# A three-stage decoder layer on one Trainium2 core: six cross-attention units in the last self-attention batch, the loop over key heads written out, and the maxima of heads 6 and 7 ahead of the rotations

## The chip, the cores and the metric

The kernel runs on one core of a Trainium2 chip. The metric is the device time of one execution in microseconds (us). The engines are PE (TensorE, the matrix engine), DVE (VectorE), ACT (ScalarE), POOL (GpSimd) and SP (SyncE, which here only issues transfers). Each runs its own list of instructions in order; they wait for each other at semaphores.

## The reference, cut to what matters

The input x is 8 sequences of 128 tokens by 512 features; ctx has the same shape.

```python
x = x + self_attention(layernorm(x))            # 32 query heads, 8 key heads of 16, causal, rotary positions
x = x + cross_attention(layernorm(x), ctx)      # keys and values from concat(ctx, latents): 256 keys
                                                # 32 query heads, 4 key heads of 128
x = x + ffn(layernorm(x))                       # up/ReLU^2/down, plus a latent path times the two best gates
```

In the cross-attention, `q = latents @ Wq`, `k, v = concat(ctx, latents) @ Wk, Wv`, a softmax over 256 keys, the sum over values, and `@ Wo`. Everything is float32. The kernel splits each operand into a high and a low part and makes three products (high by high, high by low, low by high).

## The kernel before, in words

**The split.** `split3` (lines 218 to 220) issues the three matmuls of one product. A result in a PSUM bank is turned into its two parts by ACT (`hi`, a copy, line 1033) and then DVE (`lo`, the difference, line 1280); weights that come from memory get their low part on POOL (`lo_part`, line 496). So a product that feeds another one passes PE, ACT, DVE, PE.

**Stage one, self-attention.** `batch(b, last)` on each engine runs eight batches. A batch goes over eight key heads j: `turn(j)` transposes the normalised probabilities Pa on PE (line 713), ACT and DVE split them into PTah and PTal, `values(j)` multiplies by the values on PE. Ahead of that, `scores(b, m)` makes the scores of two heads (mask by identity at line 681, then Kbdh by QTh, Kbdh by QTl, Kbdl by QTh at lines 685, 687, 690), DVE takes the maxima (`maxima`, line 1401), ACT the exponentials (`probs`, line 1088), DVE the reciprocals of the sums (`reciprocals_a`, line 1407), POOL multiplies (`normalise`, line 505). Inside batch b the queries and keys of batch b + 1 are made: `q_product`, `kv_product`, the rotary rotation on DVE (`rope_q`, lines 1339 to 1348, `rope_k_parts`, `rope_k_sum`, line 1358), `turn_qk`, and the block diagonal of the keys (Kbdh on POOL, line 490, Kbdl on DVE, line 1376). At the end of a batch the output product with SOh, the residual (line 1453), the second layer norm (xn2, line 1459) and `turn_latents` (line 650), whose result enters the tile XT.

**Units.** A "unit" is one 128 x 512 block of keys or values for the cross-attention: twelve matmuls on PE (`unit`), a copy (`unit_hi`) and a difference (`unit_lo`) into one of four slots of KVst, and a store to kv_scratch by SP (`store_unit`, two transfers). There are 32: units with part 0 need only the context, those with part 1 need latents, v of batch b only those of b, k those of four batches. The list UNITS gives their order and bank: five at the start, two in each batch (after head 0 and after the output product), and the eleven of `U_END` behind the last batch.

**Between the stages.** Behind batch 7 PE waits for the latents, runs the eleven units, then the first eight `queries` of cross-attention (WQh, WQl; split by `first_wq` on ACT and `first_wq_lo` on POOL), waits for the last unit's low part, and makes `scores_b(0, 0)` and `scores_b(0, 1)`.

**Stage two, cross-attention.** `group(g, last)` is run for four key heads g; g = 0 to 2 by a hardware loop (`Fori`) on each engine, g = 3 by a copy of its own. A group has 32 steps k: `scores_b(g, k + 2)`, the transposes of step k (line 925), from k = 8 on a piece of the output product of the batch before (`out_piece`), `queries` of the next pair of batches, `outputs(g, k - 1)`. ACT does in a step: PTh, `probs_b` (line 1170), `split_weights(k)` (WOh, at k = 0 twice, at k = 1 once), at odd k `queries` (Qh), `outputs` (Oh). DVE takes maxima (line 1513) and their negative (b_nb, line 1516).

**Stage three** is the feed-forward part, a loop over pairs of batches. The change does not touch it.

Of the kernel before, what the change touches and what calls it, by code (L numbers as in the profile page):

```python
# [34 lines left out]
NB = 8  # L35
# [25 lines left out]
def decoder_layer(nc, x, ctx, s_wq, s_wk, s_wv, s_wo, x_wq, x_wk, x_wv, x_wo, gate_w, up_w, down_w,  # L61
                  fc1_w, fc2_w, expert_w, gamma, beta, rope, out):
    with ExitStack() as stack:
# [239 lines left out]
        def targets(kind, i):  # L303
# [19 lines left out]
        U_END = [("v", b, None, 1, (0, 1, 7, 6)[b % 4]) for b in range(1, NB)] + [  # L323
            ("k", 1, g, 1, (0, 1, 7, 6)[g]) for g in range(XKV)]
        UNITS = U_START + U_BATCH + U_END
        NU = len(UNITS)
        U_B0, U_E0 = len(U_START), len(U_START) + len(U_BATCH)
# [14 lines left out]
        def _(sp):  # L342
# [37 lines left out]
            for n in range(U_E0 - 4):  # L380
                store_unit(n)
# [5 lines left out]
            for n in range(U_E0 - 4, U_E0):  # L387
                store_unit(n)
            sp.wait_ge(pe_pv, NB)
            sp.dma_start(gate_raw[:], gate_w.rearrange("(k p) n -> p k n", p=P)).then_inc(ld_gate, 16)  # L390
            for n in range(U_E0, U_E0 + 2):
                store_unit(n)
            stored(U_E0 + 2)
            for b in range(3):
                sp.dma_start(f32(KV[:, b, :]), kv_scratch[0, b]).then_inc(b_kv[b], 16)

            sp.wait_ge(pe_ht, NB)
# [13 lines left out]
            def group(g, last):  # L411
# [4 lines left out]
                for k in range(DUOS):  # L416
# [8 lines left out]
                    if k == 26 and not last:  # L425
                        first_loads(sp.snap(g + 1))
                    for done, gg, b in kv_loads:
                        if done == k + 1:

                            n = NB * gg + b if last else sp.snap(NB * gg + b)  # L430
                            sp.wait_ge(b_pe_pv, DUOS * g + done)
                            sp.dma_start(f32(KV[:, b % 3, :]), kv_scratch.rearrange("g b p n -> (g b) p n")[n]
                                         ).then_inc(b_kv[b % 3], 16)

            with sp.Fori(0, XKV - 1) as g:
                group(g, False)
            group(XKV - 1, True)
# [18 lines left out]
        def _(gp):  # L456
# [118 lines left out]
            with gp.Fori(0, XKV - 1) as g:  # L575
                group(g, False)
            group(XKV - 1, True)
# [18 lines left out]
        def _(pe):  # L596
# [73 lines left out]
            def scores(b, m):  # L670
# [6 lines left out]
                else:  # L677

                    pe.wait_ge(v_qkl, 2 * b + 2)
# [4 lines left out]
                for bk, rows in halves:  # L684
                    pe.matmul(bk[:], QTh[rows, m, :], Kbdh[rows, m, :], start=False, stop=False)  # L685
                for bk, rows in halves:
# [5 lines left out]
            def queries(g_count, head, pair, bk):  # L692
# [8 lines left out]
                op.then_inc(b_pe_q, 1)  # L701

            def batch(b, last):
# [31 lines left out]
                for j in range(SKV):  # L735
# [27 lines left out]
                    if j == 7 and not last:  # L763
                        turn_qk(b + 1)
                    if j >= 1:
                        values(j - 1)
                values(SKV - 1)
                if not last:

                    pe.wait_ge(a_exp, SKV * b + SKV)  # L770
                    scores(b + 1, 0)

# [8 lines left out]
                unit(U_B0 + 2 * b + 1)  # L781
# [3 lines left out]
                else:  # L785

# [917 lines left out]
```

## Time and profile before

| | us |
|---|---|
| median of 3 runs (lowest, highest) | 1091.8 (1091.32, 1091.91) |
| the profiled execution, its own time | 1089.78 |
| its span, first to last instruction | 1088.1 |

| engine | busy us | share of the span |
|---|---|---|
| PE (matmul) | 1038.0 | 95% |
| DVE | 639.1 | 59% |
| ACT | 546.5 | 50% |
| POOL | 387.0 | 36% |

In order of time: the start up to about 50 us, the eight self-attention batches to about 302, units and first queries to about 347, four cross-attention groups to about 948, the feed-forward part to the end. How to read a row of a timeline: start, duration, engine, line of the kernel, operation, output from input, shape, count; in brackets the idle time of the engine just before it and who ended it. Matmul ends are modelled: consecutive matmuls overlap in the rows, so the spacing of two starts is the time that one costs, and real waiting is a little more than the bracket says.

### The profile page before, as it was taken

Reading aid. Unit: us, or ns where it says so; the run is one execution under the profiler, and the core shown is the slowest. Engines: PE = TensorE matmul, PEld = TensorE weight load, DVE = VectorE, ACT = ScalarE, POOL = GpSimd, SP = SyncE. Lnnn points to the kernel's source line nnn. Section 1 sums busy time; section 2 is a strip of 40 time slices with the busy share of each in tenths; the row PEclk is TensorE's granted clock in tenths of the full one; section 3 lists DMA queues with packets and bytes.
Section 4 is the critical chain, followed back from the end, with each engine's and each line's share of the span. In section 5 each row is a group of like instructions: output and inputs, shape, how many; then the busy total and the mean of one; then the engine's idle time right before and its main releaser. Section 6 shows DMA issues by size and latency. Waiting matters only on the chain.

```text
span 1088.1 us, 19297 instructions
## 1 busy us (share of the span) xinstructions
PE 1038.0 (95%) x6808; PEld 920.3 (85%) x6808; DVE 639.1 (59%) x1369; ACT 546.5 (50%) x1657; POOL 387.0 (36%) x370
## 2 busy tenths in 40 slices
PE   5899999999899999998999998999999999999997
PEld 5667777776678999998999998999999999899996
DVE  5677787787524655555555554555546555655554
ACT  4566666656623645644545544546546446622221
POOL 2454444444331523423424414324316235611110
PEclk9999999999999999999999999999999999999999
DMA  9301111104164212121102302103112123200000
GB/s 329 93 25 40 39 39 40 32 13 113 39 201 129 59 31 77 50 78 51 49 30 59 107 24 59 37 30 107 59 40 59 35 73 97 78 21 19 19 20 20
DMA packets 70123, 68.64 MB, mean 63 GB/s; under 512 B 3984, under 2 KB 53904, under 8 KB 70032
## 3 DMA queue, kind: packets, MB, share of 16 engines
q1 hardware_dynamic: 70032, 67.43, 19.8%
q8 instruction: 56, 0.92, 0.4%
q14 instruction: 35, 0.29, 0.1%
HBM read 48.55 MB, written 18.87 MB: 62 GB/s over the span
## 4 chain that ended last, share of the span: by engine, by line
PE 83%; DVE 7%; ACT 5%; POOL 2%; issue 2%; DMA 1%; SPq 0%; POOLq 0%; DVEq 0%; ACTq 0%
PE bank L218 24%; PE bank L220 23%; PE bank L219 23%; PE bank L925 5%; PE bank L713 2%; PE bank L681 1%; ACT Pa L1088 1%; PE bank L685 1%; POOL Pa L505 1%; DVE PTal L1280 1%; ACT PTah L1033 1%; DVE b_nb L1516 1%; ACT Pb L1170 1%; DVE b_max L1513 1%; PE bank L690 1%
## 5 line engine op out<-in xcount | busy, mean ns | idle before, releaser
L543 POOL TENSOR_TENSOR Pb<-Pb,b_rec 128x512 f32<-128x512 f32 x128 | 133.3, 1042 | 406.0 <-DVE b_rec L1520 405.7
L218 PE MATMUL bank<-XTh,WQh 128*128 128x256 f32 x512 | 146.5, 286 | 3.8 <-DVE Ql L1280 3.8
L220 PE MATMUL bank<-XTh,WQl 128*128 128x256 f32 x512 | 145.9, 285 | 0.0
L219 PE MATMUL bank<-XTl,WQh 128*128 128x256 f32 x512 | 145.7, 285 | 0.0
L1170 ACT ACTIVATE Pb<-bank,b_nb 128x256 f32<-128x256 f32 x256 | 119.2, 471 | 30.1 <-DVE b_nb L1516 29.2
L1033 ACT ACTIVATE PTh<-bank 128x512 fp32r<-128x512 f32 x128 | 76.8, 600 | 104.8 <-PE bank L925 104.6
L1280 DVE TENSOR_TENSOR Ol<-bank,Oh 128x256 fp32r<-128x256 f32 x128 | 53.8, 420 | 117.7 <-ACT Oh L1033 117.6
L1088 ACT ACTIVATE Pa<-bank,a_nb 128x128 f32<-128x128 f32 x256 | 90.7, 372 | 51.8 <-DVE a_nb L1401 51.7
L505 POOL TENSOR_TENSOR Pa<-Pa,a_rec 128x512 f32<-128x512 f32 x64 | 70.5, 1101 | 114.5 <-DVE a_rec L1407 114.5
L218 PE MATMUL bank<-WOh,Oh 128*128 128x512 f32 x256 | 109.9, 429 | 1.0 <-DVE x_res L1530 1.0
L218 PEld LDWEIGHTS bank<-XTh,WQh 128*128 128x128 f32 x512 | 98.5, 192 | 9.5 <-DVE Ql L1280 4.8
L219 PEld LDWEIGHTS bank<-XTl,WQh 128*128 128x128 f32 x512 | 98.6, 193 | 4.6
L220 PE MATMUL bank<-WOh,Ol 128*128 128x512 f32 x256 | 101.0, 395 | 0.0
L219 PE MATMUL bank<-WOl,Oh 128*128 128x512 f32 x256 | 100.8, 394 | 0.0
L220 PEld LDWEIGHTS bank<-XTh,WQl 128*128 128x128 f32 x512 | 98.7, 193 | 0.0
L1033 ACT ACTIVATE Oh<-bank 128x256 fp32r<-128x256 f32 x128 | 49.2, 384 | 96.6 <-PE bank L220 90.5
L1280 DVE TENSOR_TENSOR Ql<-bank,Qh 128x512 fp32r<-128x512 f32 x64 | 44.3, 692 | 84.7 <-ACT Qh L1033 84.7
L1280 DVE TENSOR_TENSOR PTl<-bank,PTh 128x512 fp32r<-128x512 f32 x128 | 88.2, 689 | 9.9 <-ACT PTh L1033 1.1
L1513 DVE TENSOR_REDUCE b_max<-bank 128x2 f32<-128x512 f32 x128 | 87.2, 681 | 10.6 <-PE bank L220 10.6
L218 PE MATMUL bank<-KV,Qh 128*128 128x256 f32 x256 | 73.3, 286 | 7.1 <-issue 5.2
L925 PE MATMUL bank<-ident,Pb 128*128 128x128 f32 x512 | 76.9, 273 | 0.3 <-POOL Pb L543 0.3
L220 PE MATMUL bank<-KV,Ql 128*128 128x256 f32 x256 | 73.0, 285 | 0.0
(230 smaller groups left out, 2866.9 us busy)
## 6 DMA issues: line engine op xcount, KB each, us to landing
kv_scratch<-KVst SPq DMA_DIRECT2D x64, 256.0 KB, 3.0
KV<-kv_scratch SPq DMA_DIRECT2D x32, 512.0 KB, 3.3
raw<-in_L_xattn_Wo_dram SPq DMA_DIRECT2D x32, 256.0 KB, 3.6
raw<-in_L_xattn_Wq_dram SPq DMA_DIRECT2D x24, 256.0 KB, 4.0
cx<-in_ctx_dram SPq DMA_DIRECT2D x8, 256.0 KB, 8.6
raw_first<-in_L_xattn_Wq_dram SPq DMA_DIRECT2D x8, 256.0 KB, 4.5
raw<-in_L_ffn_up_w_dram SPq DMA_DIRECT2D x8, 256.0 KB, 4.1
raw<-in_L_ffn_down_w_dram SPq DMA_DIRECT2D x8, 256.0 KB, 2.7
```

The source lines that it names most:

```text
L218: pe.matmul(dst, lh, rh, start=start, stop=False)
L219: pe.matmul(dst, lh, rl, start=False, stop=False)
L220: return pe.matmul(dst, ll, rh, start=False, stop=stop)
L505: gp.tensor_tensor(pj, pj, a_rec[:, SG * j:SG * j + SG].unsqueeze(2).to_broadcast([P, SG, P]), ALU.mult).then_inc(g_norm, 1)
L543: gp.tensor_tensor(pk, pk, b_rec[:, k % 4, :].unsqueeze(2).to_broadcast([P, 2, KEYS]), ALU.mult).then_inc(b_g_norm, 1)
L713: op = pe.transpose(bank[5 + j % 2][:, c * P:(c + 1) * P], Pa[:, j % PS, c * P:(c + 1) * P], ident[:])
L925: op = pe.transpose(bank[3 + k % 2][:, c * KEYS + h * P:c * KEYS + (h + 1) * P], Pb[:, k % 4, h, c * P:(c + 1) * P], ident[:])
L1033: return act.activation(dst, src, ACT.Copy)
L1088: op = act.activation(Pa[:, j % PS, c * P:(c + 1) * P], bank[2 + j % 3][:, c * P:(c + 1) * P], ACT.Exp, bias=a_nb[:, h:h + 1], scale=1.0, ...
L1170: op = act.activation(Pb[:, k % 4, h, :], bank[k % 3][:, h * KEYS:(h + 1) * KEYS], ACT.Exp, bias=b_nb[:, k % 4, h:h + 1], scale=X_SCALE, a ...
L1280: return dve.tensor_tensor(dst, src, f32(hi_part), ALU.subtract)
L1513: dve.tensor_reduce(b_max[:, k % 4, :], bank[k % 3][:].rearrange("p (h k) -> p h k", h=2), AX.X, ALU.max).then_inc(b_v_mx, 1)
```

## The change: what it does, and the diff

1. `UNITS` is reordered. Of the eleven last units six (values of batches 1 to 6, part 1) now stand in batch 7, at heads 2, 4, 5, 6, 7 and after the last head (`LAST_STEPS`), in banks 0 and 1 by turns; five stay behind the batch. The stores, the loads of KV and the waits of SP follow the new order.
2. On PE the eight first queries are put between other work: heads 0 and 1 before the last `turn_latents`, 2 and 3 before the five last units, 4 and 5 before `scores_b(0, 0)`, 6 and 7 before `scores_b(0, 1)`. Waits are moved to where they are needed, on ACT and DVE likewise (the stores' end is waited for in `outputs(0, 0)`).
3. `scores_b(0, 2)` no longer waits for the first exponentials of its group.
4. The `Fori` loops over g become four written-out copies on all five engines.
5. In `group` on ACT the copy Qh stands before the weights of the step.
6. In `batch` on DVE the maxima of head 7 stand at head 3, behind those of head 6, and both ahead of the rotation; the reciprocals of heads 6 and 7 stand behind `rope_q` and `rope_k_parts`.
7. `scores` no longer waits for QTl and KTl before the mask, but for QTl before the product with it.

```diff
     ("k", 1, b, 0, 7) if b < XKV else ("k", 0, b - XKV, 1, 7))]
-U_END = [("v", b, None, 1, (0, 1, 7, 6)[b % 4]) for b in range(1, NB)] + [
-    ("k", 1, g, 1, (0, 1, 7, 6)[g]) for g in range(XKV)]
-UNITS = U_START + U_BATCH + U_END
+U_LAST = [("v", b, None, 1, (b + 1) % 2) for b in range(1, NB - 1)]
+U_END = [("v", NB - 1, None, 1, 1)] + [("k", 1, g, 1, 7 - g % 2) for g in range(XKV)]
+UNITS = U_START + U_BATCH[:-1] + U_LAST + U_BATCH[-1:] + U_END
 NU = len(UNITS)
-U_B0, U_E0 = len(U_START), len(U_START) + len(U_BATCH)
+U_B0, U_E0 = len(U_START), len(UNITS) - len(U_END)
+U_L0 = U_B0 + len(U_BATCH) - 1
+
+LAST_STEPS = {2: U_L0, 4: U_L0 + 1, 5: U_L0 + 2, 6: U_L0 + 3, 7: U_L0 + 4}
...
             sp.wait_ge(st_u[slot], stored_in(slot, count))
-    for n in range(U_E0 - 4):
+    for n in range(U_L0 - 3):
...
         sp.dma_start(raw_first[:, h, :].rearrange("p (k n) -> p k n", k=KC), wq_src(0, h)).then_inc(b_ld_first, 16)
-    for n in range(U_E0 - 4, U_E0):
+    for n in range(U_L0 - 3, U_L0 + 2):
+        store_unit(n)
+
+    stored(U_L0 + 2)
+    for b in range(3):
+        sp.dma_start(f32(KV[:, b, :]), kv_scratch[0, b]).then_inc(b_kv[b], 16)
+    for n in range(U_L0 + 2, U_L0 + 5):
...
     sp.dma_start(gate_raw[:], gate_w.rearrange("(k p) n -> p k n", p=P)).then_inc(ld_gate, 16)
+    for n in range(U_L0 + 5, U_E0):
+        store_unit(n)
+
+    sp.wait_ge(pe_ht, NB)
...
         store_unit(n)
-    stored(U_E0 + 2)
-    for b in range(3):
-        sp.dma_start(f32(KV[:, b, :]), kv_scratch[0, b]).then_inc(b_kv[b], 16)
-
-    sp.wait_ge(pe_ht, NB)
...
             if k == 26 and not last:
-                first_loads(sp.snap(g + 1))
+                first_loads(g + 1)
...
                 if done == k + 1:
-                    n = NB * gg + b if last else sp.snap(NB * gg + b)
                     sp.wait_ge(b_pe_pv, DUOS * g + done)
-                    sp.dma_start(f32(KV[:, b % 3, :]), kv_scratch.rearrange("g b p n -> (g b) p n")[n]
-                                 ).then_inc(b_kv[b % 3], 16)
-
-    with sp.Fori(0, XKV - 1) as g:
-        group(g, False)
-    group(XKV - 1, True)
+                    sp.dma_start(f32(KV[:, b % 3, :]), kv_scratch[gg, b]).then_inc(b_kv[b % 3], 16)
+
+    for g in range(XKV):
+        group(g, g == XKV - 1)
...
         split_weights(DUOS)
-    with gp.Fori(0, XKV - 1) as g:
-        group(g, False)
-    group(XKV - 1, True)
+    for g in range(XKV):
+        group(g, g == XKV - 1)
...
             pe.wait_ge(a_exp, SKV * b + 2 * m - 1)
-        else:
-
-            pe.wait_ge(v_qkl, 2 * b + 2)
...
             pe.matmul(bk[:], QTh[rows, m, :], Kbdh[rows, m, :], start=False, stop=False)
+        pe.wait_ge(v_qkl, 2 * b + 1)
...
         op.then_inc(b_pe_q, 1)
+
+    def first_queries(heads):
+        for h in heads:
+            queries(h + 1, h, 0, QBANK[h // 2])
...
                 turn_qk(b + 1)
+            if j in LAST_STEPS and last:
+                if j == 2:
+
+                    pe.wait_ge(v_htl, b)
+                unit(LAST_STEPS[j])
...
             scores(b + 1, 0)
+        else:
+            unit(U_L0 + 5)
...
             scores(b + 1, 1)
-        unit(U_B0 + 2 * b + 1)
+        unit(U_E0 - 1 if last else U_B0 + 2 * b + 1)
...
         else:
-
-            pe.wait_ge(v_htl, b)
+            first_queries((0, 1))
+
+            pe.wait_ge(v_ul, U_L0 + 5)
...
         batch(b, b == NB - 1)
-    pe.wait_ge(v_htl, 7)
-    for n in range(U_E0, U_E0 + 2):
-        unit(n)
-
-    pe.wait_ge(v_x2, NB)
-    unit(U_E0 + 2)
-    pe.wait_ge(v_htl, NB)
-    for n in range(U_E0 + 3, NU):
-        unit(n)
-
...
     pe.sem_inc(b_pe_wo, 1)
-    for h in range(XG):
-        queries(h + 1, h, 0, QBANK[h // 2])
-
-
-    pe.wait_ge(v_ul, NU)
+    first_queries((2, 3))
+    pe.wait_ge(v_htl, NB)
+    unit(U_E0)
+    unit(U_E0 + 1)
+
+    pe.wait_ge(v_x2, NB)
+    unit(U_E0 + 2)
+    unit(U_E0 + 3)
+    unit(U_E0 + 4)
+    first_queries((4, 5))
     scores_b(0, 0)
+    first_queries((6, 7))
+
+    pe.wait_ge(v_ul, U_E0 + 1)
...
                 if k + 2 < DUOS:
-                    pe.wait_ge(b_a_exp, DUOS * g + max(k, 1))
+
+                    if k:
+                        pe.wait_ge(b_a_exp, DUOS * g + k)
+                    elif g:
+                        pe.wait_ge(b_a_exp, DUOS * g - 2)
...
                     pe.wait_ge(b_v_q, 4 + 16 * g + k // 2)
+                if g == 0 and k == 0:
+
+                    pe.wait_ge(v_ul, NU)
...
             out_piece(g, NB - 1, i)
-    with pe.Fori(0, XKV - 1) as g:
-        group(g, False)
-    group(XKV - 1, True)
+    for g in range(XKV):
+        group(g, g == XKV - 1)
...
                     xn_hi(b + 1)
+            if j in LAST_STEPS and last:
+                unit_hi(LAST_STEPS[j])
...
                 first_wq(h)
-        unit_hi(U_B0 + 2 * b + 1)
+            unit_hi(U_L0 + 5)
+        unit_hi(U_E0 - 1 if last else U_B0 + 2 * b + 1)
...
            bank[bk][:].rearrange("p (h n) -> p h n", h=2)).then_inc(b_a_q, 1)
-    for h in range(4, XG):
-        first_wq(h)
-        unit_hi(U_E0 + h - 4)
-    for n in range(U_E0 + XG - 4, NU):
-        unit_hi(n)
-    for f in range(4):
-        queries(f + 1, f, 0, QBANK[f])
+    for n in range(4):
+        first_wq(4 + n)
+        unit_hi(U_E0 + n)
+    unit_hi(U_E0 + 4)
+
+    act.wait_ge(pe_u, NU)
+    queries(1, 0, 0, QBANK[0])
+    queries(2, 1, 0, QBANK[1])
+    queries(3, 2, 0, QBANK[2])
     probs_b(0, 0)
+    queries(4, 3, 0, QBANK[3])
...
     act.wait_ge(b_g_w, W0)
-
-
-    for slot in range(SLOTS):
-        act.wait_ge(st_u[slot], stored_in(slot, NU))
...
         act.wait_ge(b_pe_pv, DUOS * g + k + 1)
+        if g == 0 and k == 0:
+
+            for slot in range(SLOTS):
+                act.wait_ge(st_u[slot], stored_in(slot, NU))
...
                 probs_b(g + 1, k + 2 - DUOS)
-            split_weights(k)
...
                 queries(4 + 16 * g + k // 2 + 1, (k % XG) // 2, (k // XG + 1) % 2)
+            split_weights(k)
...
         split_weights(DUOS)
-    with act.Fori(0, XKV - 1) as g:
-        group(g, False)
-    group(XKV - 1, True)
+    for g in range(XKV):
+        group(g, g == XKV - 1)
...
         for j in range(SKV):
-            if j + 3 < SKV:
+            if j < 4:
                 maxima(b, j + 3)
+            if j == 3:
+                maxima(b, 7)
...
                     lo(PTal[:, j % 2, cols], bank[5 + j % 2][:, cols], PTah[:, j % 2, cols]).then_inc(done, 1)
-            if j + 2 < SKV:
+            if j < 4:
...
             if last:
+                if j in LAST_STEPS:
+                    unit_lo(LAST_STEPS[j])
+                if j in (3, 4):
+                    reciprocals_a(b, j + 3)
...
                 rope_q(b + 1)
+                reciprocals_a(b, 6)
...
                 rope_k_parts(b + 1)
+                reciprocals_a(b, 7)
...
             reciprocals_a(b + 1, 0)
+        else:
+            unit_lo(U_L0 + 5)
...
             diagonal_keys(b + 1, (2, 3))
-        unit_lo(U_B0 + 2 * b + 1)
+        unit_lo(U_E0 - 1 if last else U_B0 + 2 * b + 1)
...
         batch(b, b == NB - 1)
-    for n in range(U_E0, NU):
-        unit_lo(n)
-
...
                X3h[:, :, t * P:(t + 1) * P]).then_inc(c_v_x, 1)
-    for f in range(4):
-        queries(f + 1, f, 0, QBANK[f])
-    for k in range(2):
-        maxima_b(0, k)
-    for k in range(2):
-        reciprocals(0, k)
+    for n in range(U_E0, NU):
+        unit_lo(n)
+    queries(1, 0, 0, QBANK[0])
+    queries(2, 1, 0, QBANK[1])
+    maxima_b(0, 0)
+    queries(3, 2, 0, QBANK[2])
+    reciprocals(0, 0)
+    maxima_b(0, 1)
+    queries(4, 3, 0, QBANK[3])
+    reciprocals(0, 1)
...
     lo(GTl[:, :, 0:NE], gate_raw[:], GTh[:, :, 0:NE]).then_inc(c_v_g0, 1)
-    for slot in range(SLOTS):
-        dve.wait_ge(st_u[slot], stored_in(slot, NU))
-
...
         dve.wait_ge(b_a_o, DUOS * g + k + 1)
+        if g == 0 and k == 0:
+            for slot in range(SLOTS):
+                dve.wait_ge(st_u[slot], stored_in(slot, NU))
...
         residual(g, NB - 1)
-    with dve.Fori(0, XKV - 1) as g:
-        group(g, False)
-    group(XKV - 1, True)
+    for g in range(XKV):
+        group(g, g == XKV - 1)
```

## Rows read from the trace of the kernel before

**Rows 1.** The page: the busy share of PE, and the granted TensorE clock in 40 slices.
```profile
PE 1038.0 (95%) x6808; PEld 920.3 (85%) x6808; DVE 639.1 (59%) x1369; ACT 546.5 (50%) x1657; POOL 387.0 (36%) x370
...
PEclk9999999999999999999999999999999999999999
```
**Rows 2.** Timeline of PE at the end of batch 6.
```profile
258.15 0.48 PE L218 MATMUL bank<-PTah,Vbdh 128*128 128x512 f32 x1
...
259.29 0.66 PE L713 MATMUL bank<-ident,Pa 128*128 128x128 f32 x4 [0.20 <-POOL Pa L505]
...
260.24 0.50 PE L218 MATMUL bank<-PTah,Vbdh 128*128 128x512 f32 x1 [0.29 <-DVE PTal L1280]
...
261.80 0.66 PE L713 MATMUL bank<-ident,Pa 128*128 128x128 f32 x4 [0.60 <-POOL Pa L505]
...
265.22 0.70 PE L681 MATMUL bank<-mask_r,ident_r 128*128 128x512 f32 x2 [0.48 <-DVE KTl L1280]
265.85 0.50 PE L685 MATMUL bank<-Kbdh,QTh 64*128 64x512 f32 x2
```
**Rows 3.** Timeline of DVE in the same stretch.
```profile
253.16 0.69 DVE L1401 TENSOR_REDUCE a_nb<-bank 128x4 f32<-128x512 f32 x1 [1.66 <-PE bank L690]
...
254.75 0.69 DVE L1339 TENSOR_TENSOR rope_q<-bank,rope_t 128x512 f32<-128x512 f32 x1 [0.21 <-PE bank L220]
...
256.75 0.68 DVE L1401 TENSOR_REDUCE a_nb<-bank 128x4 f32<-128x512 f32 x1
...
257.94 0.17 DVE L1407 RECIPROCAL a_rec<-a_sum 128x4 f32<-128x4 f32 x1
...
259.49 0.69 DVE L1280 TENSOR_TENSOR PTal<-bank,PTah 128x512 fp32r<-128x512 f32 x1 [0.94 <-ACT PTah L1033]
260.10 0.17 DVE L1407 RECIPROCAL a_rec<-a_sum 128x4 f32<-128x4 f32 x1
```
**Rows 4.** Timelines of ACT (first row) and POOL in the same stretch.
```profile
257.46 0.37 ACT L1088 ACTIVATE Pa<-bank,a_nb 128x128 f32<-128x128 f32 x1 [1.00 <-DVE a_nb L1401]
...
258.19 1.04 POOL L505 TENSOR_TENSOR Pa<-Pa,a_rec 128x512 f32<-128x512 f32 x1 [2.54 <-DVE a_rec L1407]
...
264.15 3.55 POOL L490 TENSOR_TENSOR Kbdh<-KTh,bd_mask 128x512 fp32r<-128x512 f32 x3 [2.40 <-ACT KTh L1033]
```
**Rows 5.** Timeline of PE from batch 7 to the first group.
```profile
279.38 0.47 PE L218 MATMUL bank<-PTah,Vbdh 128*128 128x512 f32 x1
...
294.82 0.50 PE L218 MATMUL bank<-SOh,PTah 128*128 128x512 f32 x1 [1.15 <-DVE PTal L1280]
...
302.16 0.63 PE L650 MATMUL bank<-ident,xn 128*128 128x128 f32 x4 [1.57 <-DVE xn L1459]
...
347.59 0.38 PE L218 MATMUL bank<-KV,Qh 128*128 128x256 f32 x1 [1.91 <-ACT Pb L1170]
...
351.14 0.41 PE L218 MATMUL bank<-XTh,WQh 128*128 128x256 f32 x1
```
**Rows 6.** Timeline of ACT between the stages: the longest wait for a store.
```profile
325.25 0.60 ACT L1033 ACTIVATE KVst<-bank 128x512 fp32r<-128x512 f32 x1 [5.49 <-DMA kv_scratch<-KVst]
```
**Rows 7.** Timeline of PE where a group begins: g = 1, 2, 3.
```profile
503.22 0.38 PE L218 MATMUL bank<-KV,Qh 128*128 128x256 f32 x1 [1.90 <-issue]
...
658.54 0.38 PE L218 MATMUL bank<-KV,Qh 128*128 128x256 f32 x1 [3.30 <-issue]
...
811.68 0.28 PE L218 MATMUL bank<-KV,Qh 128*128 128x256 f32 x1
...
819.98 0.39 PE L218 MATMUL bank<-XTh,WQh 128*128 128x256 f32 x1 [1.09 <-DVE Ql L1280]
```
**Rows 8.** Timelines of DVE (first row) and ACT at the start of g = 3.
```profile
815.91 1.23 DVE L1516 TENSOR_SCALAR b_nb<-b_max 128x2 f32<-128x2 f32 x1
...
818.09 0.62 ACT L1033 ACTIVATE WOh<-raw 128x512 fp32r<-128x512 f32 x1
818.61 0.59 ACT L1033 ACTIVATE Qh<-bank 128x512 fp32r<-128x512 f32 x1
```

## The prediction, as it stood before the run

> **What bounds the kernel now.** I read the page first: PE is busy 95% of the span, at the full clock in every slice of the coarse view [rows 1]. So a gain must come from the 5% in which PE waits, or from stretches at the lower clock that a slice is too coarse to show; nothing in the change removes a matmul. Then I listed every row of PE's timeline with idle time in front of it. Outside the start and the last stage there are three kinds: a pattern that comes back in all of batches 0 to 6 (period 31.97 us), the way from batch 7 to the first cross-attention steps, and the beginnings of the groups. Since matmul ends are modelled, I take spacings of starts: a 512-column matmul costs 0.227 us, a 256-column one 0.12, four transposes 0.36, a unit 2.72, and what is beyond that is waiting.
>
> **Part 6 and 7, the batches.** At the end of a batch PE transposes head 6 at 259.29, waits, does the values of head 5 at 260.24, waits, transposes head 7 at 261.80 and begins the next scores at 265.22 with Kbdh only at 265.85 [rows 2]. Followed back: the transpose of head 6 waits for POOL (258.19) [rows 4], that for the reciprocal at 257.94, and that stands behind the maxima of head 7 at 256.75 and the values' low part, which stand behind the rotation begun at 254.75 [rows 3]. Head 7's exponentials begin at 257.46 [rows 4], its reciprocal at 260.10 behind a low part that waits for ACT [rows 3]. The scores of heads 6 and 7 were both there at 253.16.
>
> I walk through the new order with latencies of the same rows. The maxima of head 6 stay at 253.16, those of head 7 come at 253.76 (0.60 apart), the low part of head 3 at 254.36, the rotation at 255.04 (0.3 later, its four steps take 2.0), the reciprocal of head 6 at 257.03. POOL follows 0.25 later and needs 1.04 + 0.06 until PE may start: transpose of head 6 possible at 258.4. PE gets there at 258.15 + 0.78 = 258.93, so no wait. Head 7's exponentials run from 256.36 to about 257.85, its reciprocal at 258.2, POOL at 258.45, transpose possible at 259.6. What is late next is the low part of head 5: its transpose is at 257.79, ACT 0.63 later, DVE 0.64 after that (259.06), PE 0.75 after that: 259.81 instead of 260.24 [rows 2]. Then 0.77 of values, and head 7 is transposed at 260.58 instead of 261.80, `turn_qk` at 260.94 instead of 262.29, since the restart after a wait (0.13) goes too. kr is ready at 260.35, so it does not hold. Gain there: 1.35 us, carried to the end of the head loop. The rotation's delay of 0.3 is covered by this; without that cover it would cost 0.3.
>
> Behind it: KTh comes 1.28 earlier, so POOL's Kbdh begins at 264.15 - 1.28 = 262.87 and its first of three (3.55 / 3 = 1.18 each) [rows 4] lets PE start Kbdh by QTh at 264.11 instead of 265.85 [rows 2]: a gain of 1.74. The mask stands ahead of it from 263.24, no longer behind KTl. QTl (262.5) and Kbdl (264.5) are ready when their products come; the output product follows at 265.0 instead of 266.75. From there to the middle of the next batch PE has no wait of over 0.1 us in the old trace, and all chains start from PE, so the gain stays. **1.75 us in each of 7 batches: 12.2 us.** Bounds: 0.4 (only the mask's half of it, if the values keep their wait) to 2.3 (all the waiting of [rows 2] goes: 0.37 + 0.59 + 0.76 + 0.13 + 0.45); I take the walk's value, nearest to the rows.
>
> **Part 1 and 2, batch 7 and the way to the groups.** From the first values at 279.38 to `turn_latents` at 302.16 [rows 5] 22.78 us pass. The work in it: values 7 x 0.77 + 0.72, transposes 6 x 0.36, one pair of scores 1.55, output product 2.89, a unit 2.72, together 15.4. So 7.3 us are waiting for the chain PE, ACT, DVE, POOL, the largest pieces 1.15 for OTl and 1.57 for xn2 [rows 5]. Six units give 16.3 us of work to put in. Walked through: unit 20 runs from 280.5, the other steps follow without a wait, since each head now has 2.7 us more for its chain (about 2.5 to 3 long); the unit behind the last head covers OTl (ready 2 us before it ends); the k unit and the queries of heads 0 and 1 (2.72 + 2.9) cover the 4.44 us from the output product's end to the latents. Then two queries, five units, two queries, `scores_b(0, 0)`, two queries. The old 2.07 us and 0.43 of waiting at 347.59 and behind it [rows 5] (maxima and exponentials with nothing beside them) are covered by the queries of heads 6 and 7. New: on DVE Ql of heads 6 and 7 stands behind the maxima of `scores_b(0, 1)`, and the first queries of the group wait for it: 0.75. At step 2 I find 1.3 of waiting for Ql where 1.06 was: 0.25. Seven more changes of form at 0.08 cost 0.6. The sum: 7.3 + 2.07 + 0.43 - 0.75 - 0.25 - 0.6 = 8.2.
>
> The granted clock: after the waiting at 345.4 to 348.8 the matmuls of 256 columns are 0.21 apart instead of 0.12 (the row at 351.14 is one of them, 0.41 long instead of 0.28 [rows 5]); the records have the clock at half, 1.2 GHz, over 3.4 us, 16 matmuls, 1.5 us lost. With PE busy through the stretch I expect it to stay at 2.4 GHz. **Together 9.7 us**, bounds 5 (the clock still falls, and the wait at step 0 is 3) to 11.
>
> The moved waits: SP now waits in batch 7 for unit 21's store before it loads KV, and the stores of units 22 to 24 are queued behind. Unit 21 is stored at about 296, the three loads are issued by 298; the first that needs a slot from those stores is unit 26 at about 311 (in the old coordinates). ACT would stand in front of PTah there, but 13 us lie between. The same for the wait for all stores, moved into `outputs(0, 0)`: last store landed at about 338, needed at 344. The longest such wait was 5.49 us [rows 6], when the eleven units came one behind another; now PE has other work between them. I cost both at nothing; if the cover fails, up to that 5.49.
>
> **Part 4 and 5, the groups.** At g = 1 and 2 PE is idle 1.90 and 3.30 us [rows 7] with nothing that the profile shows as its cause; by spacings 2.06 and 3.46. At g = 3, which is reached by falling out of the loop into its own copy, the same instructions follow at 811.68 without a gap [rows 7]. So the gap belongs to the jump back. After the second one there is the same stretch at 1.2 GHz, 660.0 to 663.4, 1.5 us. All of it goes: 7.0 us. What is late next: Ql at step 2, as at g = 3 (1.33 by spacing). Its chain at g = 3: b_nb 1.23 us long on DVE, exponentials, WOh at 818.09, only then Qh at 818.61 [rows 8]. Part 5 takes 0.52 out: the three later groups have 3 x (1.33 - 0.52) = 2.4 instead of 1.33 + 1.05 + 1.33 = 3.7. WOh comes 0.5 later, but `out_piece` reads it from step 8 on only. Other odd steps have no wait of PE. **Together 8.3 us**, bounds 6.5 to 9.
>
> The row says that the gap is the loop's. The Trainium skill, page Runtime: NRT & Kernel Launch, section Instruction fetch mechanics, explains it: instructions are fetched ahead strictly in sequence, and a taken branch outside the fetched pages makes the engine wait for a fetch. By that rule, the trace agrees (no gap at 811.68).
>
> Part 3 only lifts a wait that is counted above. The start: the mask of the first scores may come earlier; no more than 0.3 us either way, taken as nothing.
>
> **The sum.** 12.2 + 9.7 + 8.3 = 30.2 us. The profiled execution took 1089.78, so 1059.6; the median of the runs is 2.0 above that execution, so **1061.6 us**.
>
> **The rivals.** (a) The rotation becomes the late one: DVE does two maxima and a reciprocal more before `turn_qk` and its chain ends last; the batches then give the mask's 0.4 only, 2.8 us for 7: 1071. For it: rope_q is 0.3 later; against: kr is ready 0.6 us before PE comes. Chance 0.15. (b) The units don't hide: a unit on PE in batch 7 delays the transpose which the next head's chain starts from, and the waiting moves on instead of going: 1061.6 + 8 = about 1070. Chance 0.06. (c) The gaps at the group borders are not the jump's and stay: 1061.6 + 7.0 = 1068.6. Chance 0.07, since g = 3 has none. (d) The first group still starts badly (Ql, clock at 1.2 GHz): 1061.6 + 3 = 1064.6. Chance 0.10. (e) Slower than before: the written-out code starves PE. The loop body is run three times from nearly the same code; written out, every step is new. A gap costs 1.90 to 3.30 [rows 7]; from 10 to 16 such gaps in the 96 steps of three groups the gain of 30.2 is lost; at one in four steps, 24 x 2.6 = 62 us, it is 1124. Against it: group 3 and the eight batches are written out already, and PE has no idle time there that is not put down to an engine. Chance 0.03.
>
> The skill's same section has the sequencer stream long code by itself, in blocks of 256 instructions, with the cost of a block mostly hidden; by it (e) does not occur, and the trace of group 3 agrees.
>
> **How the numbers follow.** The forecast has 0.59; its own range is 1058 to 1066 from the bounds of the batches and of the group start. The range of 8 in 10 takes in (a) to (d): 1056 to 1072. Within 0.2% (2.2 us, about what a measurement can tell from no change) would need that all three parts fail: 0.01. Slower 0.03, faster 0.96.
>
> **What would show it.** A period of 30.2 us from batch to batch with no wait of PE in front of the transposes of heads 6 and 7; no wait over 0.3 us between values of head 0 and the first queries in batch 7; no gap at the starts of g = 1 and 2; the clock at full from 50 us to the end; Ql still waited for, with about 0.8, at step 2. Wrong would be: a period above 31, waits on kr, or idle time "issue" inside the groups.

## The result, and the profile after

The changed kernel takes 1060.57 us in the median of 4 runs (1059.86 to 1061.62), the kernel before 1091.86 beside it (1091.32 to 1091.94): a ratio of 0.9714, interval 0.9701 to 0.9726, so 2.9% faster. The forecast was 1061.6. The profiled execution took 1060.31 us, its span is 1058.6.

The page, busy time by engine and the granted clock, as in [rows 1]:

```profile
PE 1029.4 (97%) x6808; PEld 918.2 (87%) x6808; DVE 645.4 (61%) x1369; ACT 544.7 (51%) x1657; POOL 384.6 (36%) x370
...
PEclk9999999999999999999999999999999999999999
```

PE has the same 6808 matmuls. 29.5 us of the span went: most of it was PE's waiting, and 3 us were two stretches of matmuls at the lower clock, shown below.

The timeline of PE at the end of batch 6, as in [rows 2] (the rows with line 719 are the transposes, those before were line 713; 686 was 685; ACT's copies, line 1033 before, are line 1051, and DVE's differences, line 1280 before, are line 1303):

```profile
249.05 0.48 PE L218 MATMUL bank<-PTah,Vbdh 128*128 128x512 f32 x1
249.83 0.60 PE L719 MATMUL bank<-ident,Pa 128*128 128x128 f32 x4
...
250.71 0.50 PE L218 MATMUL bank<-PTah,Vbdh 128*128 128x512 f32 x1 [0.28 <-DVE PTal L1303]
...
251.53 0.60 PE L719 MATMUL bank<-ident,Pa 128*128 128x128 f32 x4
...
254.24 0.63 PE L682 MATMUL bank<-mask_r,ident_r 128*128 128x512 f32 x2
254.91 0.50 PE L686 MATMUL bank<-Kbdh,QTh 64*128 64x512 f32 x2
```

The transposes of heads 6 and 7 no longer wait; one wait is left, for the low part of head 5, as the walk had it. From there to Kbdh are 4.20 us (254.91 - 250.71), where 5.61 were (265.85 - 260.24 in [rows 2]); the walk had 4.30. The same row stands at 220.44 in the batch before: the period is 30.27, forecast 30.2.

The timeline of DVE there, as in [rows 3]:

```profile
244.06 1.29 DVE L1424 TENSOR_REDUCE a_nb<-bank 128x4 f32<-128x512 f32 x2 [1.65 <-PE bank L692]
...
245.95 0.66 DVE L1362 TENSOR_TENSOR rope_q<-bank,rope_t 128x512 f32<-128x512 f32 x1
...
247.92 0.17 DVE L1430 RECIPROCAL a_rec<-a_sum 128x4 f32<-128x4 f32 x1
...
249.04 0.17 DVE L1430 RECIPROCAL a_rec<-a_sum 128x4 f32<-128x4 f32 x1
...
249.96 0.69 DVE L1303 TENSOR_TENSOR PTal<-bank,PTah 128x512 fp32r<-128x512 f32 x1 [0.75 <-ACT PTah L1051]
```

From the maxima of head 6 to the reciprocal of head 6 pass 3.86 us (4.78 before), to that of head 7 4.98 (6.94 before) [rows 3]. The reciprocals no longer stand behind the rotation and head 7's maxima. Ahead of the low part of head 5 DVE waits 0.75 for ACT, as it waited 0.94 in [rows 3]: that chain is what is left.

Between 250.71 and 329.07 PE's timeline has no row with idle time in front of it, where before stood those of [rows 2] behind 260.24, those of [rows 5] and eight more. The next rows with any, up to step 28 of the last group:

```profile
329.07 0.39 PE L218 MATMUL bank<-XTh,WQh 128*128 128x256 f32 x1 [0.42 <-DVE Ql L1303]
...
335.58 0.39 PE L218 MATMUL bank<-XTh,WQh 128*128 128x256 f32 x1 [0.35 <-DVE Ql L1303]
...
487.18 0.39 PE L218 MATMUL bank<-XTh,WQh 128*128 128x256 f32 x1 [0.57 <-DVE Ql L1303]
...
638.43 0.39 PE L218 MATMUL bank<-XTh,WQh 128*128 128x256 f32 x1 [0.57 <-DVE Ql L1303]
...
789.67 0.39 PE L218 MATMUL bank<-XTh,WQh 128*128 128x256 f32 x1 [0.58 <-DVE Ql L1303]
...
895.50 0.36 PE L218 MATMUL bank<-PTh,KV 128*128 128x256 f32 x1 [0.22 <-DVE Ol L1303]
...
905.43 0.47 PE L218 MATMUL bank<-WOh,Oh 128*128 128x512 f32 x1 [1.07 <-DVE x_res L1560]
```

No gap at the starts of g = 1 and 2 where [rows 7] had 1.90 and 3.30; Ql at step 2 is waited for 0.81 by spacing in three groups, as forecast. The row at 895.50 is new; the one at 905.43 was there before with 0.88.

The granted clock where it had fallen, busy time by stretch; first the kernel before, then the changed one at the same place of its own first group (columns: stretch, us, PE, PEld, DVE, ACT, POOL, clock, DMA share, GB/s):

```profile
349.40:352.80 3.40, 3.40 (x18) 3.40 (x18) 1.23 (x4) 2.55 (x7) 1.87 (x3) 0.51 0.01 2
660.00:663.40 3.40, 3.40 (x18) 3.40 (x17) 1.27 (x4) 2.54 (x7) 1.62 (x2) 0.51 0.01 2
```

```profile
335.90:339.30 3.40, 3.40 (x31) 3.40 (x30) 2.77 (x5) 1.51 (x6) 2.04 (x3) 1.00 0.63 160
```

18 matmuls in 3.4 us at 1.2 GHz, 31 at 2.4 GHz. In the changed kernel the records have the full clock from 50.2 us to 1053.8; the last 4.8 us are at half, as the last 4.8 were in the kernel before.

Where the time went, by starts of the same matmuls in the two profiled executions (us):

| stretch of PE | before | after | gain |
|---|---|---|---|
| first matmul to values of head 5, batch 0 | 60.39 | 60.21 | 0.2 |
| from there to the same of batch 6 | 191.80 | 181.62 | 10.2 |
| from there to step 2 of g = 0 | 97.46 | 84.87 | 12.6 |
| from there to step 2 of g = 1 | 153.92 | 151.60 | 2.3 |
| from there to step 2 of g = 2 | 156.55 | 151.25 | 5.3 |
| from there to step 2 of g = 3 | 151.81 | 151.24 | 0.6 |
| from there to the residual's wait (step 28) | 114.88 | 115.76 | -0.9 |
| the rest | 153.24 | 153.17 | 0.1 |

The sum is 30.3; the first matmul came 0.83 later, which leaves 29.5.

### The profile page after: what moved, and what is told of

It reads as the page before. It is cut to its first block, busy times and chain, and to the rows that moved or that the text cites. A ratio compares the mean times of both kernels' runs of the same rounds, so it can differ in the third digit from the quotient of the medians.

```text
span 1058.6 us, 18419 instructions
## 1 busy us (share of the span) xinstructions
PE 1029.4 (97%) x6808; PEld 918.2 (87%) x6808; DVE 645.4 (61%) x1369; ACT 544.7 (51%) x1657; POOL 384.6 (36%) x370
## 4 chain that ended last, share of the span: by engine, by line
PE 90%; DVE 3%; ACT 3%; issue 1%; POOL 1%; DMA 1%; SPq 0%; POOLq 0%; DVEq 0%; ACTq 0%
PE bank L218 26%; PE bank L220 25%; PE bank L219 25%; PE bank L941 5%; PE bank L719 2%; PE bank L682 1%; PE bank L686 1%; PE bank L692 1%; ACT Pb L1191 1%; DVE b_nb L1546 1%; PE bank L689 1%; DVE b_max L1543 1%; DMA rawQ<-in_L_attn_Wq_dram 1%; POOL XKl L532 1%; PE bank L611 1%
## 5 line engine op out<-in xcount | busy, mean ns | idle before, releaser
L510 POOL TENSOR_TENSOR Pa<-Pa,a_rec 128x512 f32<-128x512 f32 x64 | 67.8, 1061 | 101.6 <-DVE a_rec L1430 101.0
L218 PE MATMUL bank<-PTh,KV 128*128 128x256 f32 x256 | 72.7, 284 | 0.6 <-DVE Ol L1303 0.6
```

The lines of the kernel that those rows point to most:

```text
L218: pe.matmul(dst, lh, rh, start=start, stop=False)
L510: gp.tensor_tensor(pj, pj, a_rec[:, SG * j:SG * j + SG].unsqueeze(2).to_broadcast([P, SG, P]), ALU.mult).then_inc(g_norm, 1)
```

## The experiments

Each is compared with the kernel before on the same chip. Spacings of matmuls in the profiled execution count more than the medians for parts of a few microseconds: runs of the kernel before spread from 1088.84 to 1094.98, more than those of the changed one (1059.86 to 1061.62). The clock is part of that: beside the later kernels the fastest run of the kernel before (1088.84) had a mean granted clock of 0.995, the slowest (1094.98) 0.988. One stretch of 3.4 us at half clock lowers the mean by 0.0016 (an estimate, 1.7 us of 1090) and costs some 1.5 us, so by their clock these two runs are about four stretches apart. The kept traces show one such stretch that comes and goes, behind the output product of batch 7. The kernel before first, then the one with the loop written out on all engines but PE, whose PE instructions are the same:

```profile
294.90:298.30 3.40, 3.40 (x15) 2.78 (x16) 0.58 (x2) 1.48 (x3) 2.55 (x2) 1.00 0.03 5
```

```profile
295.70:299.10 3.40, 3.40 (x9) 2.63 (x10) 0.18 (x1) 1.47 (x3) 2.50 (x2) 0.51 0.02 5
```

It is there in the four kernels with PE's loop alone, the other engines' loops, PE's loop with the mask, and PE's loop with Qh; it is not there in the kernel before, with the order of DVE alone, with the mask alone, or with everything but the units. Each of these kernels has one trace, so a difference of 1.5 us between two of them can be this.

### The order of DVE alone

```diff
-    if j + 3 < SKV:
+    if j < 4:
         maxima(b, j + 3)
+    if j == 3:
+        maxima(b, 7)
 ...
         rope_q(b + 1)
+        reciprocals_a(b, 6)
 ...
         rope_k_parts(b + 1)
+        reciprocals_a(b, 7)
```

> The kernel before with the order of DVE alone (maxima of head 7 at head 3, reciprocals of heads 6 and 7 behind the rotations). Theory W (the walk of the prediction: the reciprocals stood behind the rotation; behind it the low part of head 5 is next): turn_qk 1.35 us earlier, of which 1.28 to 1.3 reaches the next scores, which still wait for KTl; period 31.97 - 1.3 = 30.67, 7 x 1.3 = 9.1 us, so 1082.7. Rival R (the rotation becomes the late one): period within 0.3 of 31.97, 1090 to 1092.

Measured: 1081.8 us, ratio 0.9906 (0.9885 to 0.9927). PE's timeline, two neighbouring batches:

```profile
223.33 0.50 PE L218 MATMUL bank<-PTah,Vbdh 128*128 128x512 f32 x1 [0.28 <-DVE PTal L1280]
...
227.50 0.70 PE L681 MATMUL bank<-mask_r,ident_r 128*128 128x512 f32 x2 [0.49 <-DVE KTl L1280]
...
254.05 0.50 PE L218 MATMUL bank<-PTah,Vbdh 128*128 128x512 f32 x1 [0.28 <-DVE PTal L1280]
```

The period is 30.72 (forecast 30.67), and the only waits are the two that theory W leaves. R has fallen. Seven periods give 8.75 us (1.25 each), and batch 7 gives 0.5: from its values of head 1 to the latents are 20.63 us, 21.13 before. The median's gain of 9.6 is that within 0.3. The profiled execution alone is only 5.9 faster than the one of the kernel before: the stretch with its first jump is 2.5 us longer (a gap of 3.14 in place of 1.90, and the lower clock behind it).

### The mask ahead of its waits, alone

```diff
-        else:
-            pe.wait_ge(v_qkl, 2 * b + 2)
 ...
             pe.matmul(bk[:], QTh[rows, m, :], Kbdh[rows, m, :], start=False, stop=False)
+        pe.wait_ge(v_qkl, 2 * b + 1)
```

> The kernel before with the wait of scores for QTl and KTl moved behind the mask, alone. Theory W: Kbdh by QTh waits for POOL's first Kbdh (264.15 + 1.18 + 0.06 = 265.39 instead of 265.85): 0.46 in each of 7 batches, 3.2 us, so 1088.6. Rival: Kbdl or OTl, made by DVE in its old order, end last and take it back: 0 to 1 us, 1091.

Measured: 1082.4 us, ratio 0.992 (0.9907 to 0.9934): 9.0 us, not 3.2. The batches are not the reason; their period is 31.50, 0.47 below that of before, as the walk says. The surplus is elsewhere in PE's timeline:

```profile
225.50 0.66 PE L711 MATMUL bank<-ident,Pa 128*128 128x128 f32 x4 [0.19 <-POOL Pa L505]
...
257.00 0.66 PE L711 MATMUL bank<-ident,Pa 128*128 128x128 f32 x4 [0.19 <-POOL Pa L505]
...
499.64 0.38 PE L218 MATMUL bank<-KV,Qh 128*128 128x256 f32 x1 [1.35 <-issue]
...
653.05 0.38 PE L218 MATMUL bank<-KV,Qh 128*128 128x256 f32 x1 [1.67 <-issue]
```

The gaps at the jumps were 1.90 and 3.30 in [rows 7]; here they are 1.35 and 1.67, and the clock does not fall behind the second. In the kernel with the order of DVE alone they were 3.14 and 3.31. The loop's price differs from trace to trace. From step 2 of g = 0 to that of g = 2 it makes 4.0 of the 7.3 us between this profiled execution and that of the kernel before; the batches up to step 2 of g = 0 make 3.3.

### The loop written out, on PE and on the others

```diff
-    with pe.Fori(0, XKV - 1) as g:
-        group(g, False)
-    group(XKV - 1, True)
+    for g in range(XKV):
+        group(g, g == XKV - 1)
```

> The kernel before with the loop over groups written out on PE alone. Theory L (the idle time of 1.90 and 3.30 us is PE's own jump back): no idle time of PE called issue at the starts of g = 1 and 2; but DVE and ACT jump back too, and DVE's first maxima of the group, which have only some 0.1 us to spare once PE comes without a gap, may be late by a gap of the same size, which PE meets at step 2 as a longer wait for Ql. So 4 to 7 us faster, 1085 to 1088. Rival (the gap is not the jump's): both gaps stay, 1091.8.

Measured: 1083.14 us, ratio 0.9927 (0.9909 to 0.9946). Both gaps are gone, so the cause is shown. The gain, 8.2 us by the medians, is above the 4 to 7 expected. The two profiled executions differ by 6.3: 2.2 and 4.8 in the two stretches with a jump, less 0.8 in the stretch before them, where this trace has the low clock behind the output product and that of the kernel before has not. DVE at the start of g = 1:

```profile
502.11 0.69 DVE L1529 TENSOR_TENSOR x_res<-x_res,bank 128x512 f32<-128x512 f32 x1 [3.27 <-PE bank L220]
502.82 0.69 DVE L1512 TENSOR_REDUCE b_max<-bank 128x2 f32<-128x512 f32 x1
```

These two rows of DVE stand on the two sides of DVE's own jump and follow without a gap: the feared second wait did not come. PE waits 1.08 at step 2 of g = 1 and 2, the same as at g = 3, which no jump precedes. That DVE's idle 3.27 us in front of them hid its fetch is likely, but only argued.

The same edit on DVE, ACT, POOL and SP, with PE left in its loop:

> The kernel before with the loop written out on DVE, ACT, POOL and SP, PE still looping. Theory L: PE's gaps of 1.9 and 3.3 us stay, the others' jumps were hidden under them; 1091.8 within 1 us. Rival (the gap comes from the other engines' jumps): 5 to 7 us faster, 1085 to 1087.

Measured: 1091.48 us, ratio 0.9995 (0.9983 to 1.0007): no change. Both gaps of PE are still there:

```profile
505.41 0.38 PE L218 MATMUL bank<-KV,Qh 128*128 128x256 f32 x1 [2.81 <-issue]
...
660.55 0.38 PE L218 MATMUL bank<-KV,Qh 128*128 128x256 f32 x1 [3.13 <-issue]
```

The gap is PE's own. But it is 2.81 and 3.13 here, where [rows 7] had 1.90 and 3.30, and PE's instructions are the same in both kernels: its length does not follow from PE's program alone.

### The mask, with PE's loop out of the way

The edits of the last two sections on PE in one kernel (the mask's wait moved, PE's `Fori` written out).

> The kernel before with PE's loop written out and the wait of scores moved behind the mask. The mask alone had given 9.0 us where 3.2 were expected, with shorter gaps at PE's jumps (1.35 and 1.67 in place of 1.90 and 3.30). Theory G (the surplus came from the jumps, whose gaps differ from program to program): with the jumps gone the mask gives its 3.3 us beside the kernel with PE's loop written out alone, which was 8.2 us faster than before: 11.5 us, 1080.0. Rival (the mask does more than the walk says, elsewhere): 8.2 + 9.0 = 17 us, 1074.

Measured: 1081.18 us, ratio 0.9903 (0.9885 to 0.992): 9.9 us below the kernel before. Against PE's loop alone (0.9927) that is 2.6 us more by ratios, 2.6 by the two profiled executions, where 3.3 were expected. The rival's 17 us are out: without the jumps the surplus of the mask alone does not come. That it was in the jumps is shown for the 4.0 us above; the rest of the 5.8 (9.0 less 3.2) stands in no row, and lies within what the clock makes of the runs of the kernel before.

### Qh ahead of the weights, with PE's loop out of the way

PE's `Fori` written out as above, and on ACT:

```diff
-    split_weights(k)
     if k % 2 == 1 and (k < DUOS - XG or not last):
         queries(4 + 16 * g + k // 2 + 1, (k % XG) // 2, (k // XG + 1) % 2)
+    split_weights(k)
```

> The kernel before with PE's loop written out and Qh ahead of the weights on ACT. Theory O: 0.52 us less waiting at step 2 of each of four groups, 2.1, and 0.6 lost in the last group where the weights now delay Oh: 1.5 us beyond the 8.2 of the loop, 1081.9, with waits of 0.8 by spacing at step 2. Rival (no loss in the last group): 1081.3.

Measured: 1082.28 us, ratio 0.9913 (0.9895 to 0.9932), 1.5 us below PE's loop alone by the ratios, less than their intervals, so the rows decide. PE waits 0.57 at step 2 (0.8 by spacing) in place of 1.08, and in the last group two rows are as in the changed kernel:

```profile
918.13 0.36 PE L218 MATMUL bank<-PTh,KV 128*128 128x256 f32 x1 [0.24 <-DVE Ol L1279]
...
928.07 0.47 PE L218 MATMUL bank<-WOh,Oh 128*128 128x512 f32 x1 [1.06 <-DVE x_res L1529]
```

### Everything but the units

The changed kernel with parts 1 to 3 as before; of the change this is left out, with the first queries and all waits that belong to it:

```diff
-UNITS = U_START + U_BATCH[:-1] + U_LAST + U_BATCH[-1:] + U_END
+UNITS = U_START + U_BATCH + U_END
```

> The changed kernel with parts 1 to 3 undone (units, first queries and their waits as before; loops written out, order of DVE, Qh and mask as changed). Theory W: the units' part was worth 9.7 us, so 1060.6 + 9.7 = 1070.3, with the waiting of batch 7 and the lower clock after the first scores as in the kernel before. Rival (once the other parts are in, batch 7's chains are shorter and the units bring less): 1066 or below.

Measured: 1068.66 us, ratio 0.9786 (0.9766 to 0.9805), so 8.1 us above the changed kernel by the medians, between the theory and the rival. By spacings of matmuls, from values of head 5 in batch 6 to step 2 of g = 1: 245.68 us here, 236.47 in the changed kernel, 9.2, so the theory's 9.7 is the nearer. The lower clock is back, 0.4 us behind the wait for the first exponentials (a row of PE's timeline, and the busy time of the stretch behind it):

```profile
335.82 0.39 PE L218 MATMUL bank<-KV,Qh 128*128 128x256 f32 x1 [1.83 <-ACT Pb L1165]
```

```profile
336.20:339.60 3.40, 3.40 (x18) 3.15 (x17) 1.96 (x5) 1.91 (x9) 1.88 (x2) 0.50 0.01 2
```

### What is left: three further edits

The changed kernel beside them, as the measure:

> The changed kernel once more, as the measure for the three kernels beside it: 1060.6 within 1 us.

Measured: 1060.6 us, ratio 0.9712 (0.9699 to 0.9725).

```diff
     if j == 4 and not last:
-        kv_product(range(KC))
+        kv_product(range(KC - 1))
+    if j == 5 and not last:
+        kv_product((KC - 1,))
 ...
     if j == 4:
-        rope_k_parts(b + 1)
         reciprocals_a(b, 7)
     if j == 5:
+        rope_k_parts(b + 1)
```

> The changed kernel, with the last quarter of kv_product moved behind the transpose of head 5 and the rotation of the keys behind the low part of head 5. Theory W (the 0.52 us that PE still waits in each batch is the chain transpose, high part, low part of head 5, which 0.36 us more work on PE covers): the wait falls to 0.16, 7 x 0.36 = 2.5 us, 1058.1. Rival: kr comes late, PE waits for it ahead of turn_qk instead: 1060.6 or above.

Measured: 1058.89 us, ratio 0.9695 (0.9681 to 0.9708). The mean of six periods falls from 30.27 to 29.90, 0.37 a batch, 2.6 us in seven; PE has no wait of over 0.1 us in the batches any more, for kr neither. The median moved by 1.7.

```diff
-    steps = [((0, 0, 1, 2, 3, 4, 5, 5)[h], "wo", h) for h in range(XG)]
+    steps = [((1, 2, 3, 3, 4, 4, 5, 5)[h], "wo", h) for h in range(XG)]
```

> The changed kernel with the weights of the output product split at steps 1, 2, 3, 3, 4, 4, 5, 5 of a group instead of 0, 0, 1, 2, 3, 4, 5, 5. Theory P (the b_nb of 1.23 us beside POOL's pair of WOl, where 0.17 is the rule, is what makes Ql late at step 2): b_nb short, Ql 1.06 us earlier, the waits of 0.81 at three groups and 0.57 at the first go: 3.0 us, 1057.6. Rival (the length of b_nb is not POOL's doing, or POOL's norm of step 2 stretches it as well): the waits stay, 1060.6.

Measured: 1057.89 us, ratio 0.9689 (0.9675 to 0.9702), 2.7 us below the measure. DVE at the start of g = 1:

```profile
484.64 0.17 DVE L1546 TENSOR_SCALAR b_nb<-b_max 128x2 f32<-128x2 f32 x1
...
486.41 0.69 DVE L1303 TENSOR_TENSOR Ql<-bank,Qh 128x512 fp32r<-128x512 f32 x1 [0.34 <-ACT Qh L1051]
```

b_nb takes 0.17 in place of 1.23 [rows 8], and PE has no wait at step 2 of g = 1 to 3 any more. At g = 0 its wait of 0.57 by spacing stays, so 0.5 of the 3.0 expected did not come; b_nb is 0.52 there with the pair moved as without. What sets the length of b_nb shows beside POOL (the changed kernel, behind step 2 of g = 0):

```profile
336.64 1.29 POOL L501 TENSOR_TENSOR WOl<-raw,WOh 128x512 fp32r<-128x512 f32 x1
336.69 1.26 DVE L1546 TENSOR_SCALAR b_nb<-b_max 128x2 f32<-128x2 f32 x1
```

b_nb ends at 337.95, 0.02 us after POOL's operation. So do the others: 25 of the 128 b_nb of the changed kernel take over 0.3 us, 23 in the kernel before, and each of them ends 0.02 to 0.03 us after a POOL operation that was running when it began. The 0.52 at g = 0 ends so behind POOL's multiplication of Pb.

```diff
+    if k > XG:
+        split_weights(k)
     if k % 2 == 1 and (k < DUOS - XG or not last):
         queries(...)
-    split_weights(k)
+    if k <= XG:
+        split_weights(k)
```

> The changed kernel with Qh ahead of the weights in steps 0 to 8 of a group only, behind them later as before the change. Theory O (in the last group the weights now stand between Qh and Oh, where they used to fill ACT's wait for the queries, so Oh comes late at step 24 and PE waits 0.39 and later 0.19 more): 0.6 us faster, 1060.0. Rival (these waits have another cause): no difference.

Measured: 1059.81 us, ratio 0.9709 (0.9696 to 0.9722). The median's 0.8 lies inside the intervals; by rows the wait for Ol at step 24 is gone, and the one for the residual is 1.12 by spacing, as in the kernel before, in place of 1.31. Theory O holds for the waits.

All three together:

> The changed kernel with all three further edits: the last quarter of kv_product behind the transpose of head 5, the weights split at steps 1 to 5, Qh first in steps 0 to 8 only. Theory: they touch different waits and add: 2.5 + 2.8 + 0.6 = 5.9 us below 1060.6, so 1054.7. Rival (what is late next takes part of it back): 1056 to 1058.

Measured: 1053.76 us (1052.96 to 1055.2), ratio 0.9654 (0.9634 to 0.9673), so 3.5% below the kernel before and 6 to 7 below the changed kernel. PE's waits of over 0.1 us from 50 us to step 28 of the last group are then three, two at g = 0 and the one for the residual:

```profile
325.46 0.39 PE L218 MATMUL bank<-XTh,WQh 128*128 128x256 f32 x1 [0.42 <-DVE Ql L1308]
...
331.93 0.39 PE L218 MATMUL bank<-XTh,WQh 128*128 128x256 f32 x1 [0.31 <-DVE Ql L1308]
...
898.10 0.47 PE L218 MATMUL bank<-WOh,Oh 128*128 128x512 f32 x1 [0.88 <-DVE x_res L1565]
```

Behind these rows two short ones are left in the last group (0.34 and 0.15), as in the kernel before.

## Why the prediction was right, point by point

**The batches.** Forecast 12.2; measured 10.2 for six periods (1.70 each) and about 1.5 for the seventh and the start together, 11.7. The walk named the next late thing (the low part of head 5, 0.52 by spacing) and both halves of the gain: alone they shorten the period by 1.25 and 0.47, together 1.70. The edit of `kv_product` (0.37 less wait for 0.36 more work) confirms the length of the chain that is left.

**Batch 7 and the way to the groups.** Forecast 9.7. In the table it is the 12.6 less 1.3 for the rest of batch 6: 11.3. Against everything else it is worth 9.2. The difference is no error of the units: the order of DVE shortens batch 7 by 0.5 by itself, and without the units, but with Qh early, PE has no wait at step 2 of g = 0 at all, where the kernel before had 0.81 (1.06 by spacing). So Qh, costed under the groups, helps at g = 0 as well. Two terms were mis-sized. The new wait at step 2 of g = 0 was put at 1.3 and is 0.57, because I let b_nb take over 1 us as in [rows 8]; it is 0.52 there, and POOL's pair starts behind it. And the 0.6 for changes of form I find in no row. The wait at step 0 was put at 0.75 and is 0.66 by spacing. The clock stayed up, as said, until 1053.8 us. No store was waited for: ACT's waits in front of KVst name only PE, where [rows 6] had 5.49.

**The groups.** Forecast 8.3; the last four stretches of groups give 2.3 + 5.3 + 0.6 - 0.9 = 7.3. The jumps are right, and they are PE's alone. The step that failed is the pair of sentences that put part 5 at no cost beyond step 2: WOh is read from step 8 on only, and "Other odd steps have no wait of PE." I looked at what reads the weights and at the steps with a wait, not at what is queued behind the weights on ACT. In step 23 of the last group two chunks now stand between Qh and Oh:

```profile
888.77 0.60 ACT L1051 ACTIVATE Qh<-bank 128x512 fp32r<-128x512 f32 x1 [0.80 <-PE bank L220]
889.27 0.63 ACT L1051 ACTIVATE UPh<-raw 128x512 fp32r<-128x512 f32 x1
889.79 0.62 ACT L1051 ACTIVATE F1h<-raw 128x512 fp32r<-128x512 f32 x1
890.31 0.38 ACT L1051 ACTIVATE Oh<-bank 128x256 fp32r<-128x256 f32 x1
```

ACT idles 0.80 ahead of Qh, where the chunks used to be, and everything behind it on ACT slides. With Qh first in steps 0 to 8 only, the stretch from step 2 of g = 3 to the residual's wait is 114.88 us again, as in the kernel before, in place of 115.76: the whole 0.9 was this.

**The rivals.** (a), late rotations: out, by the order of DVE alone. (b), units that don't hide: out, PE has no idle row in batch 7. (c), gaps that are not the jump's: out, by PE's loop alone. (e), starved code: out, no idle time called issue within the groups. Of (d) the two waits at g = 0 are left, 1.2 us in all.

The errors went both ways and nearly cancel: -0.5, +1.6, -1.0 against 30.2. The margin of 1 us between forecast and median is luck beside such terms. One more term was wrong and hidden by them: the 2.0 us by which the median of the kernel before lies above its profiled execution was carried over. In the changed kernel it is 0.3 (1060.57 and 1060.31). Without it the forecast was 1059.6 for an execution of 1060.31; the sum of the stretches held (30.3 against 30.2), and the first matmul came 0.83 later. Why the 2.0 did not carry over is in part argued: without the jumps and with the clock up between the stages, less is left in which executions can differ.

## What to carry to other kernels

List the bottleneck engine's waits one by one, and for each walk the chain with the durations and latencies of the trace until something else is late: that gave the period to 0.1 us. When an instruction is moved in a queue, look at everything behind it in that queue, in every variant of the loop, and at what used to fill the wait in front of its new place. A hardware loop around a long body on the bottleneck engine cost it a gap of 1.35 to 3.31 us at each jump back here, and a comparison of two kernels that both loop carries those gaps, and the stretches of lower clock that come and go, as noise of several microseconds. So add up stretches between the same matmuls before believing a median.

## What the runs showed of the hardware that was not expected

The gap at PE's jump back is no constant: 1.35, 1.67, 1.90, 2.81, 3.13, 3.14, 3.30 and 3.31 us were seen in the traces of four kernels with the same loop, two of which have the same PE instructions; why they differ, and whether they differ between executions of one kernel, is open. DVE's and ACT's jumps cost nothing visible in the kernel in which only PE's loop is written out. The negation of the maxima on DVE (b_nb, 128 x 2 elements) takes 0.17 us in most steps and up to 1.26 when it begins during a POOL operation: every one of over 0.3 us ends 0.02 to 0.03 us after that operation, so what counts is how much of it is left. With POOL's pair moved away it is 0.17 again (g = 1 to 3); at steps where one of POOL's operations still overlaps it, it is up to 0.97 in that kernel as well.
